# A transformer layer with routed attention and eight gated experts: the small LoRA product of the expert output moved behind the output matmuls

## The chip, the cores and the metric

The kernel runs on all 8 cores of one Trainium2 chip. Each core computes one of the eight sequences of the batch, 2048 tokens of width 1024, with the same program and no traffic between cores. The metric is the device time in microseconds of the slowest core.

## The reference

```python
x = x + attn(layernorm(x), ...)          # windowed light attention plus routed heavy attention
x = x + ffn(layernorm(x), Wg, W1, b1, A1, B1, W2, b2, A2, B2, W3, b3, A3, B3)

def ffn(x, ...):
    scores = softmax(xf @ Wg.T)
    expert_weights, expert_indices = top_k(scores, 2)   # normalised to sum 1
    gates = (one_hot(expert_indices, 8) * expert_weights[..., None]).sum(axis=1)
    h1 = lora_in(xf, W1, b1, A1, B1)     # xf @ W1^T + (xf @ A1^T) @ B1^T + b1, all 8 experts
    h3 = lora_in(xf, W3, b3, A3, B3)
    g = silu(h1) * h3
    y_e = lora_out(g, W2, b2, A2, B2)    # g @ W2^T + (g @ A2^T) @ B2^T + b2
    return einsum('te,ted->td', gates, y_e)
```

There are 8 experts with 2048 hidden units each, and every expert is computed for every token; the gates are zero for six of the eight. The rank of the LoRA parts is 16.

## The kernel before, in words

Everything is kept transposed, with features on the partitions and tokens along the free axis. Programs for the five engines are written out by hand: `P.do(engine, ...)` appends an instruction to that engine's queue, each engine runs its queue in order, and semaphores given as `waits` hold an instruction until another engine has counted up. With `drain=True` the next instruction of the same queue also waits for the end of this one. So the order in the text is the order on each engine.

The change lies in the last part, the expert stage (block "g"). Its outer loop `eq_i` runs over 32 quarters: 8 experts `e` with 4 quarters `q` of 512 hidden units each. The weights of a quarter (w1b, w3b, w2b, 1 MB each as bf16, and small LoRA pieces) are in two buffers that take turns; POOL's queue issues those of the next quarter when `mm4` says that the quarter that last used the buffer is done. In a quarter the loop `tc` runs over 4 chunks of 512 tokens. One pass of it is called a tile here; there are 128.

A tile does, in this order on TensorE:

- in quarter 0 only: the rank-16 products with A1 and A3 (`mku`, L1302) into rows 0 to 15 of the PSUM bank pMISC, which VectorE copies to u1sb and u3sb (L1315, L1320). The first of them waits for `vec3` among others.
- the gate matmul (L1324) into chunk 3 of pSIM. It waits for `oe`, that is for all sums into x1 so far. VectorE copies the result to gateb (L1330).
- four times (`hc`): a w1 group of eight matmuls and one for the LoRA part (`h13`, L1341 and L1346), and a w3 group of the same kind. ScalarE applies Silu to the one (L1356) and the bias to the other (L1365); VectorE multiplies them (L1370) and multiplies by gateb into gTq (L1376).
- the u2 product (`u2mm`, L1383): four matmuls of gTq with a2tqb, 16 wide, into rows 32 to 47 of pMISC. VectorE adds that to u2sb (L1391), which runs over the four quarters of an expert; in quarter 3 it is also copied to bf16 as u2bf (L1398).
- eight y groups (`ymm`, L1409): `dc` runs over the output features, 4 matmuls of w2b with gTq each, into chunks 0 and 1 of pSIM in turn. In quarter 3 each group has one more matmul that uses u2bf (L1415). After each group VectorE adds the chunk into x1 (L1432, "the sum into x1"); a y group waits until all but the last of these sums are done, by `oe`.

The first y group of every tile waits for `vec3`, so for the u2sb sum of its own tile. u2bf is read in quarter 3 alone.

Of the kernel before, what the change touches and what calls it, by code (L numbers as in the profile page):

```python
# [10 lines left out]
ALU = mybir.AluOpType  # L11
# [154 lines left out]
def build(debug_taps=()):  # L166
# [156 lines left out]
    u2sb = rowt("u2sb", 32, 0, 16, 2048, F32, ROWS)  # L323
    u2bf = rowt("u2bf", 0, 4096, 16, 2048, BF16, ROWS)
# [19 lines left out]
    pMISC = nc.alloc_psum_tensor("pMISC", [128, 512], F32)  # L344
# [8 lines left out]
    S = {k: Sem(nc, k) for k in names}  # L353
    nc.const_aps.register(F32, 1e-5, fconst[0:1, 0:1])
    P = Prog(nc, S)
# [27 lines left out]
    for _e in ("tensor", "vector", "scalar", "gpsimd"):  # L383
        P.do(_e, lambda E: E.nop(),
             waits=[(S["sdc"], SD_CONST), (S["sgc"], S["sgc"].n)])
# [41 lines left out]
    for dc in range(8):  # L427
# [3 lines left out]
             waits=ld + [(S["mm"], S["mm"].n)], inc=S["scl"], drain=True)  # L431
        def mk(d=dc):
            def f(E):
# [12 lines left out]
             inc=S["mm"])  # L446
# [5 lines left out]
    for dc in range(8):  # L452
# [3 lines left out]
             waits=ld + [(S["scl"], S["scl"].n),  # L456
                         (S["mm"], max(0, S["mm"].n - 1))],
             inc=S["vec"], drain=True)
        P.do("vector", (lambda d=dc: lambda E:
                        E.tensor_mul(xlch(d)[:, :], xlch(d)[:, :], rB[:, :]))(),  # L460
             inc=S["vec"], drain=True)
        P.do("scalar", (lambda d=dc: lambda E:
                        E.activation(xsq[:, :], xlch(d)[:, :], AF.Square))(),
             waits=[(S["vec"], S["vec"].n), (S["mm"], S["mm"].n)],
             inc=S["scl"], drain=True)
        def mk(d=dc):
# [19 lines left out]
         waits=[(S["mm"], S["mm"].n)], inc=S["vec"], drain=True)  # L486
    P.do("vector", lambda E: E.tensor_scalar_mul(c0_row, pSIM[0:1, 0:2048], 1 / 1024.0),
         inc=S["vec"], drain=True)
    P.do("vector", lambda E: E.tensor_copy(sr_row, pSIM[32:33, 0:2048]),
         inc=S["vec"], drain=True)  # L490
    P.do("vector", lambda E: E.tensor_mul(c1_row, c0_row, c0_row),
         inc=S["vec"], drain=True)
# [4 lines left out]
         waits=[(S["vec"], S["vec"].n)], inc=S["scl"], drain=True)  # L497
    P.do("scalar", lambda E: E.activation(sr_row, sr_row, AF.Sqrt),
         inc=S["scl"], drain=True)
    P.do("vector", lambda E: E.reciprocal(c1_row, t_row),  # L500
         waits=[(S["scl"], S["scl"].n)], inc=S["vec"], drain=True)
    P.do("vector", lambda E: E.tensor_scalar_max(sr_row, sr_row, 1e-12),
         inc=S["vec"], drain=True)
    P.do("vector", lambda E: E.reciprocal(sr_row, sr_row), inc=S["vec"], drain=True)
    P.do("vector", lambda E: E.tensor_scalar_mul(sr_row, sr_row, 32.0),
         inc=S["vec"], drain=True)
    P.do("vector", lambda E: E.tensor_mul(c0_row, c0_row, c1_row),
         inc=S["vec"], drain=True)
    P.do("vector", lambda E: E.tensor_scalar_mul(c0_row, c0_row, -1.0),
         inc=S["vec"], drain=True)  # L510
# [6 lines left out]
    for dc in range(8):  # L517
# [3 lines left out]
             waits=ld + [(S["scl"], S["scl"].n)], inc=S["vec"], drain=True)  # L521
        P.do("vector", lambda E: E.tensor_mul(xlt[:, :], xlt[:, :], rB[:, :]),
             inc=S["vec"], drain=True)
        P.do("vector", lambda E: E.tensor_mul(xlt[:, :], xlt[:, :], c1B[:, :]),
             inc=S["vec"], drain=True)
        P.do("vector", lambda E: E.tensor_add(xlt[:, :], xlt[:, :], c0B[:, :]),
             inc=S["vec"], drain=True)
# [4 lines left out]
             inc=S["vec"], drain=True)  # L532
    P.flush("p2b")
    if "ln2T" in debug_taps:
# [4 lines left out]
          inc=S["sgw"])  # L539
# [4 lines left out]
    for tt in range(16):  # L544
        def mk(tt=tt):
            def f(E):
# [10 lines left out]
             inc=S["mm"])  # L557
# [3 lines left out]
             waits=[(S["mm"], S["mm"].n)], inc=S["vec3"], drain=True)  # L561
# [3 lines left out]
             inc=S["vec2"], drain=True)  # L565
    for fc in range(8):
# [4 lines left out]
              waits=[(S["mm2"], max(0, S["mm2"].n - 4)), (S["mm"], S["mm"].n)],  # L571
              inc=wsem)
        sgn = wsem.n
        for tc in range(4):
            k = 4 * fc + tc
            def mk(fc=fc, tc=tc, k=k):
                def f(E):
# [12 lines left out]
                 inc=S["mm2"])  # L590
# [8 lines left out]
    if "lqkv" in debug_taps:  # L599
# [3 lines left out]
         waits=[(S["vec"], S["vec"].n)], inc=S["pool"], drain=True)  # L603
# [684 lines left out]
    for eq_i in range(32):  # L1288
# [7 lines left out]
        for tc in range(4):  # L1296
# [37 lines left out]
            for hc in range(4):  # L1334
# [3 lines left out]
                def h13(wb, btq, usb, bank, tc=tc, hc=hc):  # L1338
                    def f(E):
# [36 lines left out]
                                E.tensor_mul(gTq[:, 512 * hc:512 * hc + 512],  # L1376
                                             gtmp1[:, :], gateb[:, :]))(),
                     inc=S["vec"], drain=True)
            def u2mm(par=par):
                def f(E):  # L1380
                    ins = None
                    for hc in range(4):
                        ins = E.matmul(pMISC[32:48, 0:512],  # L1383
                                       a2tqb[par][:, 16 * hc:16 * hc + 16],
                                       gTq[:, 512 * hc:512 * hc + 512],
                                       start=(hc == 0), stop=(hc == 3))
                    return ins
                return f
            P.do("tensor", u2mm(), waits=[(S["vec"], S["vec"].n)], inc=S["mm2"])
            P.do("vector", (lambda tc=tc: lambda E:  # L1390
                            E.scalar_tensor_tensor(u2sb[:, 512 * tc:512 * tc + 512],  # L1391
                                                   pMISC[32:48, 0:512], 1.0,
                                                   u2sb[:, 512 * tc:512 * tc + 512],
                                                   ALU.mult, ALU.add))(),
                 waits=[(S["mm2"], S["mm2"].n)], inc=S["vec3"], drain=True)
            if q == 3:
                P.do("vector", (lambda tc=tc: lambda E:
                                E.tensor_copy(u2bf[:, 512 * tc:512 * tc + 512],  # L1398
                                              u2sb[:, 512 * tc:512 * tc + 512]))(),
                     inc=S["vec3"], drain=True)  # L1400
            GTC = S["vec"].n
            for dc in range(8):
                ybank = 0 if dc % 2 == 0 else 1
                def ymm(dc=dc, tc=tc, par=par, q=q, eq_i=eq_i, yb=ybank):
                    def f(E):
                        ins = None
                        for hc in range(4):
                            last = (hc == 3) and q != 3 and eq_i != 3
                            ins = E.matmul(pch(yb),  # L1409
                                           w2b[par][:, 1024 * hc + 128 * dc:  # L1410
                                                    1024 * hc + 128 * dc + 128],
                                           gTq[:, 512 * hc:512 * hc + 512],
                                           start=(hc == 0), stop=last)
                        if q == 3:
                            ins = E.matmul(pch(yb),  # L1415
                                           b2te[:, 128 * dc:128 * dc + 128],
                                           u2bf[:, 512 * tc:512 * tc + 512],
                                           start=False, stop=(eq_i != 3))
                        if eq_i == 3:
                            ins = E.matmul(pch(yb),  # L1420
                                           b2allb[:, 128 * dc:128 * dc + 128],
                                           gatesF[:, 512 * tc:512 * tc + 512],
                                           start=False, stop=True)
                        return ins
                    return f
                P.do("tensor", ymm(),
                     waits=[(S["vec"], GTC), (S["vec3"], S["vec3"].n),
                            (S["oe"], max(0, S["oe"].n - 1)),
                            (S["scl"], S["scl"].n), (S["scl2"], S["scl2"].n)],
                     inc=S["av"])  # L1430
                P.do("vector", (lambda dc=dc, tc=tc, yb=ybank: lambda E:
                                E.scalar_tensor_tensor(  # L1432
                                    x1[:, 2048 * dc + 512 * tc:
                                       2048 * dc + 512 * tc + 512],
                                    pch(yb), 1.0,
                                    x1[:, 2048 * dc + 512 * tc:
                                       2048 * dc + 512 * tc + 512],
                                    ALU.mult, ALU.add))(),
                     waits=[(S["av"], S["av"].n)], inc=S["oe"], drain=True)
        P.do("tensor", lambda E: E.nop(),  # L1440
             waits=[(S["scl"], S["scl"].n), (S["scl2"], S["scl2"].n),
                    (S["mm2"], S["mm2"].n), (S["av"], S["av"].n)],
# [36 lines left out]
```

How the kernel before makes its waits and increments, by code:

```python
                    def body(E):  # L145
                        seen = {}
                        prev_pend = [None]
                        for (waits, emit, inch, k, pend) in ops:
                            allw = list(waits)
                            if prev_pend[0] is not None:
                                allw.append(prev_pend[0])
                            for (s, n) in allw:
                                h = s.h
                                if seen.get(id(h), -1) < n:
                                    E.wait_ge(h, n)
                                    seen[id(h)] = n
                            ins = emit(E)
                            if inch is not None:
                                ins.then_inc(inch, k)
                            prev_pend[0] = (pend[0], pend[1]) if pend else None
```

## Time and profile before

| | us |
|---|---|
| median of 2 runs | 9090.02 (9080.91 to 9099.13) |
| the profiled execution | 8785.57 |
| its span, slowest core (core 2) | 8784.0 |
| its span, fastest core (core 7) | 8736.2 |
| expert stage in it (4142.5 to the end) | 4642 |

The profile is taken on the slowest core. Its page gives busy time by engine and by slices of the span; the trace behind it can be asked for waits (who stood idle, and whose end let it go on), for the instructions in order of time, and for the TensorE clock that was granted in a stretch (1.00 is 2.4 GHz, 0.50 is 1.2 GHz).

### The profile page before, as it was taken

The numbers are of one execution on the slowest core, as the hardware profiler recorded it, in microseconds if no ns is written. First come the engines' busy times: TensorE is split into PE (matmuls) and PEld (weight loads), VectorE is DVE, ScalarE is ACT, GpSimd is POOL, SyncE is SP. The second block draws the span as 40 slices with busy tenths as digits, with TensorE's granted clock in tenths as the row PEclk, the third lists the DMA queues.
The fourth block names the chain that finished last, engine by engine and source line by source line (L and its number), as shares of the span: only waits on it lengthen the run. The fifth ranks groups of instructions, "written<-read, shape, count | busy, mean of one in ns | idle before, by whom it ended". The sixth has DMA issues, their size and how long they took to land.

```text
span 8784.0 us, 70962 instructions; the slowest of 8 cores (8736.2 to 8784.0 us)
## 1 busy us (share of the span) xinstructions
PE 5469.5 (62%) x21893; PEld 2092.0 (24%) x22208; DVE 3297.3 (38%) x5936; ACT 1409.5 (16%) x1819; POOL 305.1 (3%) x335
## 2 busy tenths in 40 slices
PE   5221122245555555541888888888888888888887
PEld 1010000013333333210322322222223223232222
DVE  2732744474444444324322332323333323233322
ACT  1012000002222222111111111111111111111111
POOL 0022000000000000000000000000000000000000
PEclk8565555575555555675987989989999899899988
DMA  2100000010000000102011111121211021111110
GB/s 89 44 9 0 0 0 0 30 23 1 1 1 1 1 1 1 48 0 30 15 30 16 26 19 25 21 30 15 30 16 30 15 30 24 21 23 22 26 19 39
DMA packets 149539, 169.20 MB, mean 19 GB/s; under 512 B 55972, under 2 KB 125092, under 8 KB 142772
## 3 DMA queue, kind: packets, MB, share of 16 engines
q0 software_dynamic: 140512, 111.61, 8.7%
q1 hardware_dynamic: 8660, 53.04, 1.7%
q8 instruction: 189, 3.10, 0.1%
q14 instruction: 178, 1.46, 0.1%
HBM read 267.67 MB, written 8.39 MB: 31 GB/s over the span
## 4 chain that ended last, share of the span: by engine, by line
PE 43%; DVE 5%; issue 3%; ACT 1%; DMA 1%; DVEq 0%; POOL 0%; ACTq 0%; PEldq 0%; POOLq 0%
PE pSIM L1341 21%; PE pSIM L1409 12%; PE pSIM L1346 4%; DVE x L1432 2%; PE pMISC L1383 2%; PE pMISC L1302 2%; PE pSIM L1415 1%; ACT gtmp L1365 1%; DVE u2sb L1391 1%; DVE gtmp L1370 1%; DVE gTq L1376 1%; DMA b3ce<-b3c 1%; PE pSIM L1324 0%; DVEq L155 0%; DVE u1sb L1315 0%
## 5 line engine op out<-in xcount | busy, mean ns | idle before, releaser
L1409 PE MATMUL pSIM<-gTq,w2b 128*128 128x512 bf16 x4001 | 1236.0, 456 | 224.6 <-DVE u2sb L1391 125.6
L1432 DVE SCALAR_TENSOR_TENSOR x<-pSIM,x 128x512 f32<-128x512 f32 x1024 | 708.5, 692 | 837.3 <-PE pSIM L1409 491.3
L1341 PE MATMUL pSIM<-xl2T,w1b 128*128 128x512 bf16 x3989 | 977.3, 386 | 31.6 <-DVE u3sb L1320 23.2
L1341 PE MATMUL pSIM<-xl2T,w3b 128*128 128x512 bf16 x4005 | 971.5, 383 | 7.1 <-issue 3.5
L1370 DVE TENSOR_TENSOR gtmp<-gtmp,gtmp 128x512 bf16<-128x512 bf16 x512 | 217.8, 425 | 1893.7 <-ACT gtmp L1365 1893.7
L1356 ACT ACTIVATE gtmp<-pSIM,b1ce 128x512 bf16<-128x512 f32 x512 | 351.8, 687 | 3165.7 <-PE pSIM L1346 3147.3
L1409 PEld LDWEIGHTS pSIM<-gTq,w2b 128*128 128x128 bf16 x4096 | 396.7, 110 | 1019.6 <-issue 859.7
L969 PE MATMUL pT<-idbf,attnbf 128*128 128x128 bf16 x2048 | 259.0, 307 | 592.3 <-ACT attnbf L953 567.2
L1341 PEld LDWEIGHTS pSIM<-xl2T,w1b 128*128 128x128 bf16 x4096 | 362.7, 98 | 516.1 <-issue 172.6
L1341 PEld LDWEIGHTS pSIM<-xl2T,w3b 128*128 128x128 bf16 x4096 | 360.0, 98 | 485.3 <-issue 137.2
L1365 ACT ACTIVATE gtmp<-pSIM,b3ce 128x512 bf16<-128x512 f32 x512 | 352.0, 688 | 726.8 <-PE pSIM L1346 726.8
L940 DVE TENSOR_REDUCE smwk<-pSIM 128x1 f32<-128x512 f32 x512 | 354.2, 692 | 55.9 <-PE pSIM L924 2.3
L969 PEld LDWEIGHTS pT<-idbf,attnbf 128*128 128x128 bf16 x2048 | 198.4, 139 | 679.3 <-issue 679.3
L1383 PE MATMUL pMISC<-gTq,a2tqb 128*16 128x512 bf16 x512 | 170.7, 467 | 271.1 <-DVE gTq L1376 271.1
L953 ACT ACTIVATE attnbf<-pSIM,smwk 128x1024 bf16<-128x1024 f32 x128 | 142.6, 1114 | 1137.2 <-DVE smwk L949 1137.2
L757 PE MATMUL pT<-idbf,lattnT 128*128 128x128 bf16 x128 | 33.8, 264 | 426.9 <-DVE lattnT L752 426.9
L983 DVE COPY attnT<-pT 128x1024 bf16<-128x1024 bf16 x128 | 88.5, 692 | 497.1 <-PE pT L969 497.1
L995 PE MATMUL pOUT<-attnT,hv 128*65 128x128 bf16 x2048 | 245.0, 313 | 0.1
L1376 DVE TENSOR_TENSOR gTq<-gtmp,gateb 128x512 bf16<-128x512 bf16 x512 | 217.7, 425 | 53.3
L924 PE MATMUL pSIM<-hk,hq 64*128 64x512 bf16 x512 | 234.6, 609 | 4.7 <-DVE selqb L910 4.7
L995 PEld LDWEIGHTS pOUT<-attnT,hv 128*65 128x65 bf16 x2048 | 215.0, 174 | 19.0 <-issue 1.2
L413 PE MATMUL pSIM<-key_rt,ones_f 1*128 1x512 f32 x8 | 7.2, 1072 | 334.2 <-DVE zp_rt L646 334.2
(262 smaller groups left out, 4834.8 us busy)
## 6 DMA issues: line engine op xcount, KB each, us to landing
w1b<-w1q POOLq DMA_DIRECT2D x32, 1024.0 KB, 11.0
w3b<-w3q POOLq DMA_DIRECT2D x32, 1024.0 KB, 15.2
w2b<-w2q POOLq DMA_DIRECT2D x32, 1024.0 KB, 18.2
xs<-xT SPq DMA_DIRECT2D x24, 1024.0 KB, 4.9
xc<-xT SPq DMA_DIRECT2D x16, 1024.0 KB, 5.7
out<-x SPq DMA_DIRECT2D x8, 1024.0 KB, 10.4
wst<-wqkv POOLq DMA_DIRECT2D x8, 256.0 KB, 4.5
cos<-cos SPq DMA_DIRECT2D x1, 1024.0 KB
```

Source lines behind the costliest of these rows:

```text
L940: E.reduce_max(smwk[:, 2 + kc:3 + kc], pSIM[:, 512 * kc:512 * kc + 512], axis=AX.X))(),
L969: ins = E.transpose(pT[:, 1024 * half + 128 * (j - j0): 1024 * half + 128 * (j - j0) + 128], attnbf[:, 128 * j:128 * j + 128], idbf[:, :])
L995: ins = E.matmul(pOUT[0:65, 0:128], hv[:, 520 * j + 65 * h:520 * j + 65 * h + 65], attnT[:, 128 * j:128 * j + 128], start=(start and j == ...
L1341: E.matmul(pSIM[:, 512 * bank:512 * bank + 512], wb[:, 512 * dc + 128 * hc:512 * dc + 128 * hc + 128], xl2T[:, 2048 * dc + 512 * tc: 2048 ...
L1346: return E.matmul(pSIM[:, 512 * bank:512 * bank + 512], btq[:, 128 * hc:128 * hc + 128], usb[:, 512 * tc:512 * tc + 512], start=False, sto ...
L1356: E.activation(gtmp1[:, :], pSIM[:, 512 * b:512 * b + 512], AF.Silu, bias=b1ce[:, hcg:hcg + 1], scale=1.0))(),
L1365: E.activation(gtmp2[:, :], pSIM[:, 512 * b:512 * b + 512], AF.Identity, bias=b3ce[:, hcg:hcg + 1], scale=1.0))(),
L1370: P.do("vector", lambda E: E.tensor_mul(gtmp1[:, :], gtmp1[:, :], gtmp2[:, :]), waits=[(S["scl"], S["scl"].n), (S["scl2"], S["scl2"].n), ( ...
L1376: E.tensor_mul(gTq[:, 512 * hc:512 * hc + 512], gtmp1[:, :], gateb[:, :]))(),
L1383: ins = E.matmul(pMISC[32:48, 0:512], a2tqb[par][:, 16 * hc:16 * hc + 16], gTq[:, 512 * hc:512 * hc + 512], start=(hc == 0), stop=(hc == 3))
L1409: ins = E.matmul(pch(yb), w2b[par][:, 1024 * hc + 128 * dc: 1024 * hc + 128 * dc + 128], gTq[:, 512 * hc:512 * hc + 512], start=(hc == 0), ...
L1432: E.scalar_tensor_tensor(x1[:, 2048 * dc + 512 * tc: 2048 * dc + 512 * tc + 512], pch(yb), 1.0, x1[:, 2048 * dc + 512 * tc: 2048 * dc + 51 ...
```

## The change

In quarters 0, 1 and 2 the u2 product and the u2sb sum are issued behind the eight y groups and their sums into x1, and the y groups no longer wait for `vec3`. In quarter 3 they stay in front, with the wait. The u2 product keeps its count to wait for (`GTC`, the last gTq of its tile). The lines that follow move down: L1391 becomes L1394, L1409 becomes L1415, L1415 becomes L1421 and L1432 becomes L1438.

```diff
-            P.do("tensor", u2mm(), waits=[(S["vec"], S["vec"].n)], inc=S["mm2"])
-            P.do("vector", ... u2sb sum ...
-                 waits=[(S["mm2"], S["mm2"].n)], inc=S["vec3"], drain=True)
+            GTC = S["vec"].n
+
+            def emit_u2(tc=tc, par=par, q=q):
+                P.do("tensor", u2mm(par), waits=[(S["vec"], GTC)], inc=S["mm2"])
+                P.do("vector", ... u2sb sum ...
+                     waits=[(S["mm2"], S["mm2"].n)], inc=S["vec3"], drain=True)
+                if q == 3:
+                    P.do("vector", ... copy to u2bf ..., inc=S["vec3"], drain=True)
+
             if q == 3:
-                P.do("vector", ... copy to u2bf ..., inc=S["vec3"], drain=True)
-            GTC = S["vec"].n
+                emit_u2()
             for dc in range(8):
...
-                P.do("tensor", ymm(),
-                     waits=[(S["vec"], GTC), (S["vec3"], S["vec3"].n),
-                            (S["oe"], max(0, S["oe"].n - 1)),
-                            (S["scl"], S["scl"].n), (S["scl2"], S["scl2"].n)],
-                     inc=S["av"])
+                yw = [(S["vec"], GTC), (S["oe"], max(0, S["oe"].n - 1)),
+                      (S["scl"], S["scl"].n), (S["scl2"], S["scl2"].n)]
+                if q == 3:
+                    yw.append((S["vec3"], S["vec3"].n))
+                P.do("tensor", ymm(), waits=yw, inc=S["av"])
                 P.do("vector", ... sum into x1 ...)
+            if q != 3:
+                emit_u2()
```

On TensorE, between the first and the second tile of the first quarter 0 (the other quarters 0 are the same):

```order
 L1341 MATMUL pSIM<-xl2T,w3b_165 128x512 x8
 L1346 MATMUL pSIM<-u3sb,b3tqb_151 128x512
-L1383 MATMUL pMISC<-gTq,a2tqb_153 16x512 x4
-L1409 MATMUL pSIM<-gTq,w2b_167 128x512 x32
+L1415 MATMUL pSIM<-gTq,w2b_167 128x512 x32
+L1383 MATMUL pMISC<-gTq,a2tqb_153 16x512 x4
 L1302 MATMUL pMISC<-xl2T,a1te 16x512 x8
 L1302 MATMUL pMISC<-xl2T,a3te 16x512 x8
```

The u2 product stands behind the 32 matmuls of y, and directly in front of the a1 product of the next tile, which uses the same PSUM bank and waits for `vec3`.

On TensorE at the end of a tile of quarter 1, before:

```order
L1346 MATMUL pSIM<-u3sb,b3tqb_152 128x512
L1383 MATMUL pMISC<-gTq,a2tqb_154 16x512 x4
L1409 MATMUL pSIM<-gTq,w2b_168 128x512 x32
L1324 MATMUL pSIM<-gatesF,sel_55 128x512
L1341 MATMUL pSIM<-xl2T,w1b_164 128x512 x8
```

and after:

```order
L1346 MATMUL pSIM<-u3sb,b3tqb_152 128x512
L1415 MATMUL pSIM<-gTq,w2b_168 128x512 x32
L1383 MATMUL pMISC<-gTq,a2tqb_154 16x512 x4
L1324 MATMUL pSIM<-gatesF,sel_55 128x512
L1341 MATMUL pSIM<-xl2T,w1b_164 128x512 x8
```

Here the u2 product stands between the last y and the gate matmul.

On VectorE around the end of a tile of quarter 1, before:

```order
L1376 TENSOR_TENSOR gTq<-gtmp_121,gateb 128x512
L1391 SCALAR_TENSOR_TENSOR u2sb<-pMISC,u2sb 16x512
L1432 SCALAR_TENSOR_TENSOR x_111<-pSIM,x_111 128x512 x8
L1330 CAST gateb<-pSIM 128x512
L1370 TENSOR_TENSOR gtmp_121<-gtmp_121,gtmp_122 128x512
```

and after:

```order
L1376 TENSOR_TENSOR gTq<-gtmp_121,gateb 128x512
L1438 SCALAR_TENSOR_TENSOR x_111<-pSIM,x_111 128x512 x8
L1394 SCALAR_TENSOR_TENSOR u2sb<-pMISC,u2sb 16x512
L1330 CAST gateb<-pSIM 128x512
L1370 TENSOR_TENSOR gtmp_121<-gtmp_121,gtmp_122 128x512
```

The u2sb sum stands between the last sum into x1 and the gateb copy of the next tile. ScalarE's and POOL's instructions are in the same order in both kernels.

## Rows read from the trace of the kernel before

**Rows 1.** Page: busy tenths in 40 slices, and the last chain by line.
```profile
PE   5221122245555555541888888888888888888887
...
DVE  2732744474444444324322332323333323233322
...
PE pSIM L1341 21%; PE pSIM L1409 12%; PE pSIM L1346 4%; DVE x L1432 2%; PE pMISC L1383 2%; PE pMISC L1302 2%; PE pSIM L1415 1%; ACT gtmp L1365 1%; DVE u2sb L1391 1%; DVE gtmp L1370 1%; DVE gTq L1376 1%; DMA b3ce<-b3c 1%; PE pSIM L1324 0%; DVEq L155 0%; DVE u1sb L1315 0%
```

**Rows 2.** Spans and mean granted clock, slowest and fastest core.
```profile
core 2: 8784.0 us, clock 0.737
...
core 7: 8736.2 us, clock 0.740
```

**Rows 3.** TensorE's waits, 4142.5 to 8785: total us, times, longest us.
```profile
PE pMISC L1383 <- DVE gTq L1376: 271.1, 128, 2.5
PE pSIM L1409 <- DVE u2sb L1391: 125.6, 96, 2.0
PE pSIM L1324 <- DVE x L1432: 98.0, 96, 1.4
PE pSIM L1409 <- DVE u2bf L1398: 59.2, 32, 2.5
```

**Rows 4.** Timeline around one tile's end: start, us, instruction, [idle before <-releaser].
```profile
5727.72 1.02 PE L1383 MATMUL pMISC<-gTq,a2tqb 128*16 128x512 bf16 x4 [2.11 <-DVE gTq L1376]
5728.92 0.68 DVE L1391 SCALAR_TENSOR_TENSOR u2sb<-pMISC,u2sb 16x512 f32<-16x512 f32 x1 [1.35 <-PE pMISC L1383]
...
5729.97 2.72 PE L1409 MATMUL pSIM<-gTq,w2b 128*128 128x512 bf16 x6 [1.22 <-DVE u2sb L1391]
...
5739.66 0.69 DVE L1432 SCALAR_TENSOR_TENSOR x<-pSIM,x 128x512 f32<-128x512 f32 x1 [0.48 <-PE pSIM L1409]
...
5740.49 0.37 PE L1324 MATMUL pSIM<-gatesF,sel 8*128 8x512 bf16 x1 [1.01 <-DVE x L1432]
...
5740.80 1.90 PE L1341 MATMUL pSIM<-xl2T,w1b 128*128 128x512 bf16 x8
5741.04 0.69 DVE L1330 CAST gateb<-pSIM 128x512 bf16<-128x512 f32 x1 [0.69 <-PE pSIM L1324]
...
5742.95 0.39 PE L1341 MATMUL pSIM<-xl2T,w3b 128*128 128x512 bf16 x1
```

**Rows 5.** Stretches: us, busy of five engines (count), granted clock, DMA share, GB/s.
```profile
4142.50:8785.00 4642.50, 3901.03 (x14442) 1333.98 (x14735) 1387.61 (x2405) 705.07 (x1025) 153.90 (x215) 0.89 0.15 23
...
5475.60:5607.40 131.80, 111.87 (x428) 39.76 (x437) 41.25 (x72) 22.00 (x32) 4.34 (x7) 0.92 0.16 25
5607.40:5740.50 133.10, 113.00 (x428) 40.02 (x437) 41.23 (x72) 22.00 (x32) 4.37 (x7) 0.91 0.16 25
...
8464.30:8614.10 149.80, 131.06 (x428) 42.88 (x437) 41.25 (x72) 21.99 (x32) 4.05 (x6) 0.76 0.13 22
8464.30:8487.40 23.10, 20.90 (x72) 6.96 (x74) 4.09 (x9) 5.50 (x8) 4.05 (x6) 0.81 0.85 139
...
5730.00:5733.50 3.50, 3.28 (x9) 1.28 (x11) 0.69 (x1) 0.00 (x0) 0.00 (x0) 0.56 0.00 0
...
5738.00:5740.50 2.50, 1.34 (x7) 0.36 (x5) 1.69 (x3) 0.00 (x0) 0.29 (x1) 1.00 0.00 0
```

**Rows 6.** Timeline of TensorE in a tile that keeps its clock.
```profile
6034.07 1.02 PE L1383 MATMUL pMISC<-gTq,a2tqb 128*16 128x512 bf16 x4 [2.11 <-DVE gTq L1376]
6036.31 1.89 PE L1409 MATMUL pSIM<-gTq,w2b 128*128 128x512 bf16 x7 [1.22 <-DVE u2sb L1391]
...
6045.68 0.37 PE L1324 MATMUL pSIM<-gatesF,sel 8*128 8x512 bf16 x1 [1.01 <-DVE x L1432]
```

**Rows 7.** Timeline where a tile of quarter 0 follows another.
```profile
6007.97 1.02 PE L1409 MATMUL pSIM<-gTq,w2b 128*128 128x512 bf16 x4
...
6008.93 1.89 PE L1302 MATMUL pMISC<-xl2T,a1te 128*16 128x512 bf16 x8
6009.17 0.69 DVE L1432 SCALAR_TENSOR_TENSOR x<-pSIM,x 128x512 f32<-128x512 f32 x1 [0.48 <-PE pSIM L1409]
```

More of the change, by code:

```diff
@@ L1378, in build, with u2mm @@
                      inc=S["vec"], drain=True)
-            def u2mm(par=par):
+            def u2mm(par):
                 def f(E):
@@ L1388, in u2mm @@
                 return f
-            P.do("tensor", u2mm(), waits=[(S["vec"], S["vec"].n)], inc=S["mm2"])
[L1390 to L1394, printed above, removed]
-                 waits=[(S["mm2"], S["mm2"].n)], inc=S["vec3"], drain=True)
-            if q == 3:
[L1397 to L1400, printed above, removed]
-            GTC = S["vec"].n
+            GTC = S["vec"].n
+            def emit_u2(tc=tc, par=par, q=q):
+                P.do("tensor", u2mm(par), waits=[(S["vec"], GTC)], inc=S["mm2"])
+                P.do("vector", (lambda tc=tc: lambda E:
+                                E.scalar_tensor_tensor(
+                                    u2sb[:, 512 * tc:512 * tc + 512],
+                                    pMISC[32:48, 0:512], 1.0,
+                                    u2sb[:, 512 * tc:512 * tc + 512],
+                                    ALU.mult, ALU.add))(),
+                     waits=[(S["mm2"], S["mm2"].n)], inc=S["vec3"], drain=True)
+                if q == 3:
+                    P.do("vector", (lambda tc=tc: lambda E:
+                                    E.tensor_copy(u2bf[:, 512 * tc:512 * tc + 512],
+                                                  u2sb[:, 512 * tc:512 * tc + 512]))(),
+                         inc=S["vec3"], drain=True)
+            if q == 3:
+                emit_u2()
             for dc in range(8):
```

## The prediction

> **What bounds the kernel now.** I read the page first. From slice 20 of its 40 slices on TensorE is busy about eight tenths and VectorE two to four, and the chain that ended last runs mostly over TensorE, by the expert stage's lines L1341, L1409, L1346, L1383 and over the sum into x1, L1432 [rows 1]. The slowest core spans 8784.0 us and the cores agree within 0.6%, so one stands for all [rows 2]. Then TensorE's list of waits over the expert stage, 4142.5 to 8785: its two largest are both around the small u2 product. It waits for the last gTq in front of L1383, 271.1 us in 128 times, and for the u2sb sum in front of L1409, 125.6 us in 96 times [rows 3]. The 96 are the tiles of quarters 0 to 2 (8 experts x 3 quarters x 4 token chunks), which are the tiles that the change touches. Third is the wait of the next tile's gate matmul for the last sum into x1, 98.0 us, 96 times.
>
> The timeline of one tile (gate matmul at 5708.0) shows the order: last w3 group until 5725.6 (u2 starts at 5727.72 after 2.11 idle), idle 2.11 while ScalarE and VectorE finish gTq, u2 product at 5727.72, idle 1.22 for the u2sb sum, first y at 5729.97, eight y groups, last sum into x1 at 5739.66, next gate at 5740.49 [rows 4]. Last I read the granted clock by stretches. It is 1.00 (2.4 GHz) up to the u2 product (its four matmuls take 1.02 us in this tile and in that of [rows 6]), falls to 1.2 GHz behind it (the mean of 5730 to 5733.5 is 0.56, and L1409 needs 2.72 us for six matmuls there), and is 1.00 again at the tile's end [rows 4, 5]. In another tile it didn't fall: first y 6036.31, next gate 6045.68 [rows 6]. So the gap around u2 costs twice: its own length, and a y stage at the lower clock behind it.
>
> **The change, part by part.** In quarters 0 to 2 the four u2 matmuls and the u2sb sum move behind the eight y groups, and y no longer waits for the sum. In quarter 3 all stays.
>
> *In front of y, 96 tiles.* The first y now starts where L1383 did: 5729.97 - 5727.72 = 2.25 us earlier [rows 4], and 6036.31 - 6034.07 = 2.24 in the other tile [rows 6]. The wait for gTq in front of it stays (2.11 us), since y reads gTq too; it is what is late next. 96 x 2.25 = 216 us.
>
> *Behind y, 72 tiles that are followed by a gate matmul.* The four u2 matmuls take about 4 x 0.22 = 0.9 us at 2.4 GHz. They start when the last y ends, and TensorE already stands idle 1.01 us there until the last sum into x1 is done, as the gate matmul waits for it in both kernels [rows 4, 6]. That idle time hides them, with about 0.1 us to spare; without the cover they would cost 0.9. The u2sb sum (0.68 us) is then queued on VectorE between the last sum into x1, done at 5740.35, and the gateb copy: it would run to about 5741.13 and the copy (0.69) to about 5741.9, where it ended at 5741.73. The first that needs gateb is the w3 group, behind a w1 group, at 5742.95, and so isn't held [rows 4]. Cost 0. From both sides: nothing, or 0.3 us x 72 = 22 us if u2 ends late.
>
> *Behind y, 24 tiles of quarter 0 that are followed by the a1 product of the next chunk.* Before, a1 follows the last y without a gap: L1409 at 6007.97 for 1.02, L1302 at 6008.93 [rows 7]. Now it waits for the u2sb sum, because both use pMISC. The last sum into x1 ends at 6009.86, the u2sb sum after it takes 0.68 and some 0.1 to start, and a matmul starts 0.37 after such a sum (5729.60 to 5729.97, [rows 4]): a1 at about 6011.0, 2.1 us later than before. 24 x 2.1 = 50 us are given back. Queued behind the waiting a1 is all of TensorE's work; VectorE waits for a1.
>
> *The clock.* Mean length of a tile of quarters 1 and 2 of one expert: (131.8 + 133.1) / 8 = 33.1 us [rows 5]; 21.95 us from the gate to the first y (5708.0 to 5729.97), so y to the next gate takes 11.15. It takes 9.37 where the clock stays at 2.4 GHz [rows 6], 10.52 where it falls briefly (5729.97 to 5740.49) [rows 4], and the mean says that longer falls are common. The lower clock thus costs some 1.8 us a tile. No row shows the new gap. The nearest on one side is the old gap, 2.11 idle, 1.0 of work, 1.22 idle: the clock falls after it. On the other side is the idle 1.01 in front of the gate matmul, after which it stays (1.00 in 5738 to 5740.5) [rows 5]. The new one, 2.11 idle and then full work, lies between. I take half of the tiles without a fall and half with the short one: 9.37 + 0.5 x 1.15 = 9.95, a gain of 1.2 x 96 = 115 us. Ends: nothing (every tile falls as now) and 1.8 x 96 = 173 us (none falls).
>
> Sum: 216 - 50 + 115 = 281 us, ends 216 - 50 - 22 = 144 and 216 - 50 + 173 = 339.
>
> *Which time it is taken from.* The profiled execution took 8785.57 us, so the sum gives 8505 for such a run. The two runs shown are 9081 to 9099, median 9090.02: 304 us or 3.5% more. One state in the trace could make this: from 8464.3 on the slowest core was granted 0.81, and the four tiles to 8614.1 took 149.8 us (mean 0.76, with the falls in them), 37.45 each, 4.3 more than 33.1 [rows 5]; 304 / 4.3 = 71 tiles in it would do. That is an estimate; the trace can't tell. The gap in front of u2 is set by ScalarE and VectorE and not by that clock, so I take the same 281 us off: 9090 - 281 = 8809.
>
> The Trainium skill ("TensorE: Matmul & The Clock Gate", section "Seeing it yourself") says that a current limit takes a die to 13/16 of the clock once three of its cores run dense matmuls, and holds it while the load lasts. This case's trace agrees on the level, 0.81, but shows it for a short stretch only, with the mean of the expert stage at 0.89, falls to 1.2 GHz included. By the rule all 128 tiles would be in it before and after, and the gain would be about the same; but a kernel with fewer gaps is denser, which is the third rival.
>
> **Rivals.**
>
> *1. The clock still falls in every tile as now.* For: even two idle pieces of 2.1 and 1.2 with work between them bring it down nearly always, and the larger piece stays. Against: between the pieces only 1.0 us of work stood, now full work follows at once. Gain 216 - 50 = 166 us: 8924.
>
> *2. It falls in none.* For: tiles exist that didn't fall with the whole gap [rows 6]. Against: those are few, by the mean of 11.15 against 9.37. Gain 339 us: 8751.
>
> *3. The denser kernel sits longer at the 0.81 clock (the slower side).* Place: the w1 and w3 groups, whose pitch goes from 0.22 to 0.26 us. Price 4.3 us a tile [rows 5]. It eats the 281 us from 66 more tiles on. If 71 tiles are in it already, the other 57 cost 245 us: 9054, within 2%. If the 304 us come from something else and 124 tiles are new in it, 533 us: 9342. For: TensorE's share of work in a tile rises by some 12%. Against: quarters with TensorE busy 85% of the time (111.87 of 131.8 us) show a mean of 0.92, which leaves no room for it [rows 5], and the cores differ little [rows 2].
>
> That the change doesn't do what it says is no rival: the order of TensorE's instructions shows u2 behind y, and the wait of y for the u2sb sum is gone.
>
> **How the numbers follow.** Forecast 0.66, rival 1 0.14, rival 2 0.12, rival 3 0.08, half of it slower. A measurement of this kernel tells about 2% (182 us) from no change. Faster by over 2%: forecast, rival 2, and a little of rival 1 where some tiles keep the clock, 0.66 + 0.12 + 0.02 = 0.80. Slower by over 2%: half of rival 3, 0.04. Within 2%: 0.16. The range reaches from 8700 (339 us, and another 0.3 us x 96 for y stages a little shorter than 9.37, 368 us in all, rounded down) to 8950 (the low end of the sum, 144 us, gives 8946).
>
> **What would show it.** Right: TensorE's wait for u2sb in front of y is gone in 96 tiles and only the one for u2bf (32 times, 59.2 us [rows 3]) stays; the wait for gTq, about 200 us, stands in front of y instead of in front of u2; a new wait for u2sb stands in front of L1302, at most 2.1 us in each of 24 times; the mean clock of the expert stage is over 0.89 and its length about 4643 - 281 = 4362 us; tiles of quarters 1 and 2 take 29.0 to 30.5 us. Wrong: a mean clock that stays at 0.89 or below (rival 1), a gate matmul that starts later than 1.0 us after the last y, or much more time at 0.81 (rival 3).

## The result, and the profile after

| | before | changed |
|---|---|---|
| median of all runs, us | 8914.52 (10 runs, 8779.12 to 9099.13) | 8582.01 (11 runs, 8549.66 to 8839.43) |
| profiled execution, span of the slowest core, us | 8784.0 | 8560.0 |
| expert stage in it, us | 4642 | 4421 |

The ratio is 0.9735, 95% interval 0.9692 to 0.9778: 2.65% faster. In the profiled executions it is 224 us, 221 of them in the expert stage. The forecast said faster by 281 us and a time of 8809 in a range of 8700 to 8950. The direction came out and the mechanism in kind; the gain was 0.8 of the forecast, and the time is below the range. In some executions of either kernel the cores of one die, or of both, are granted a lower clock (in the changed kernel's run of 8839 us 0.711 against 0.747 on the other die), and the ratios here are of the executions without that, so they differ from the ratio of the medians in the table. The two runs of before that were at hand for the prediction, 9081 and 9099, are the longest of its ten; the shortest four are 8779 to 8794.

TensorE's waits in the expert stage of the changed kernel (total us, times, longest us), beside [rows 3]:

```profile
PE pSIM L1415 <- DVE gTq L1376: 224.7, 96, 2.7
PE pMISC L1383 <- DVE gTq L1376: 67.9, 32, 2.5
PE pSIM L1415 <- DVE u2bf L1402: 49.5, 32, 1.9
...
PE pMISC L1302 <- DVE u2sb L1394: 26.7, 24, 1.1
PE pSIM L1324 <- DVE x L1438: 25.5, 27, 1.0
```

The 96 waits of y for the u2sb sum are gone and only the 32 for u2bf are left. The wait for gTq stands in front of y in 96 tiles, at 224.7 / 96 = 2.34 us each, where in front of u2 it was 271.1 / 128 = 2.12. The wait for u2bf in quarter 3, which should have stayed as it was, fell from 59.2 to 49.5 us; the experiment on the waits of y says why. The new wait in front of a1 (L1302) is there, 24 times, 1.1 us each. And the gate matmul's wait for the last sum into x1 shrank from 98.0 us in 96 times to 25.5 in 27: that is the idle time in which u2 now hides.

TensorE's timeline of the changed kernel at the end of a tile of quarter 2, and where a tile of quarter 0 follows another (beside [rows 4, 7]):

```profile
5557.66 1.02 PE L1415 MATMUL pSIM<-gTq,w2b 128*128 128x512 bf16 x4
5558.61 1.03 PE L1383 MATMUL pMISC<-gTq,a2tqb 128*16 128x512 bf16 x4
5559.70 0.37 PE L1324 MATMUL pSIM<-gatesF,sel 8*128 8x512 bf16 x1
5560.00 1.90 PE L1341 MATMUL pSIM<-xl2T,w1b 128*128 128x512 bf16 x8
...
5871.17 1.89 PE L1415 MATMUL pSIM<-gTq,w2b 128*128 128x512 bf16 x8 [2.33 <-DVE gTq L1376]
...
5879.10 1.03 PE L1383 MATMUL pMISC<-gTq,a2tqb 128*16 128x512 bf16 x4
5881.24 1.89 PE L1302 MATMUL pMISC<-xl2T,a1te 128*16 128x512 bf16 x8 [1.11 <-DVE u2sb L1394]
```

In front of the gate matmul nothing is idle any more. In quarter 0 a1 starts 5881.24 - 5879.10 = 2.14 us behind the start of u2, and before it started there itself: the 2.1 us that the prediction gives back.

The stretches of the changed kernel: the expert stage, then quarters 1 and 2 of the third expert (us, busy of five engines, granted clock, DMA share, GB/s), beside [rows 5]:

```profile
4138.70:8560.00 4421.30, 3859.36 (x14737) 1320.20 (x14736) 1387.64 (x2406) 705.06 (x1025) 153.89 (x215) 0.91 0.15 24
5409.00:5529.40 120.40, 109.36 (x437) 38.98 (x437) 41.29 (x73) 22.00 (x32) 4.33 (x6) 0.96 0.17 27
5529.40:5652.10 122.70, 110.88 (x436) 39.03 (x437) 41.19 (x73) 22.00 (x32) 4.34 (x6) 0.94 0.17 27
```

The two quarters take (120.4 + 122.7) / 8 = 30.4 us a tile; they took 33.1, and the sum of the prediction makes 33.1 - 2.25 - 1.2 = 29.65 of them. The granted clock rose from 0.92 and 0.91 to 0.96 and 0.94, not to 1.00. So the clock still falls in these tiles, for a shorter time. That is the open point with which the experiments began.

### The profile page after: what moved, and what is told of

The parts are those of the page before. It is cut to its first block, busy times and chain, and to the rows that moved or that the text cites. A ratio compares the mean times of both kernels' runs of the same rounds, so it can differ in the third digit from the quotient of the medians.

```text
span 8560.0 us, 71205 instructions; the slowest of 8 cores (8515.9 to 8560.0 us)
## 1 busy us (share of the span) xinstructions
PE 5425.2 (63%) x22208; PEld 2076.7 (24%) x22208; DVE 3296.0 (39%) x5936; ACT 1409.5 (16%) x1819; POOL 305.1 (4%) x335
## 4 chain that ended last, share of the span: by engine, by line
PE 43%; DVE 4%; issue 2%; ACT 1%; DMA 1%; POOL 0%; DVEq 0%; ACTq 0%; PEldq 0%; POOLq 0%
PE pSIM L1341 22%; PE pSIM L1415 12%; PE pSIM L1346 4%; PE pMISC L1302 2%; PE pMISC L1383 2%; DVE x L1438 2%; PE pSIM L1421 1%; ACT gtmp L1365 1%; DVE gtmp L1370 1%; DVE gTq L1376 1%; DMA b3ce<-b3c 1%; DVE u2sb L1394 0%; PE pSIM L1324 0%; DVE u3sb L1320 0%; DVE u1sb L1315 0%
## 5 line engine op out<-in xcount | busy, mean ns | idle before, releaser
L1415 PE MATMUL pSIM<-gTq,w2b 128*128 128x512 bf16 x4096 | 1196.8, 440 | 305.5 <-DVE gTq L1376 224.7
L1341 PE MATMUL pSIM<-xl2T,w1b 128*128 128x512 bf16 x4096 | 999.9, 388 | 21.0 <-DVE u3sb L1320 21.0
L1438 DVE SCALAR_TENSOR_TENSOR x<-pSIM,x 128x512 f32<-128x512 f32 x1024 | 708.0, 691 | 767.3 <-PE pSIM L1415 450.8
L1341 PE MATMUL pSIM<-xl2T,w3b 128*128 128x512 bf16 x4096 | 980.0, 382 | 0.0
L1415 PEld LDWEIGHTS pSIM<-gTq,w2b 128*128 128x128 bf16 x4096 | 385.1, 107 | 1039.7 <-issue 852.5
L1341 PEld LDWEIGHTS pSIM<-xl2T,w1b 128*128 128x128 bf16 x4096 | 364.1, 99 | 520.0 <-issue 179.5
L1341 PEld LDWEIGHTS pSIM<-xl2T,w3b 128*128 128x128 bf16 x4096 | 359.7, 98 | 485.8 <-issue 136.4
L1346 PE MATMUL pSIM<-u1sb,b1tqb 16*128 16x512 bf16 x512 | 200.0, 391 | 0.0
```

The source lines that it names most:

```text
L1341: E.matmul(pSIM[:, 512 * bank:512 * bank + 512], wb[:, 512 * dc + 128 * hc:512 * dc + 128 * hc + 128], xl2T[:, 2048 * dc + 512 * tc: 2048 ...
L1346: return E.matmul(pSIM[:, 512 * bank:512 * bank + 512], btq[:, 128 * hc:128 * hc + 128], usb[:, 512 * tc:512 * tc + 512], start=False, sto ...
L1415: ins = E.matmul(pch(yb), w2b[par][:, 1024 * hc + 128 * dc: 1024 * hc + 128 * dc + 128], gTq[:, 512 * hc:512 * hc + 512], start=(hc == 0), ...
L1438: E.scalar_tensor_tensor(x1[:, 2048 * dc + 512 * tc: 2048 * dc + 512 * tc + 512], pch(yb), 1.0, x1[:, 2048 * dc + 512 * tc: 2048 * dc + 51 ...
```

## The experiments

All ratios are to the kernel before on the same chip. "Unused matmuls" are extra ones whose result nobody reads; apart from them the experiments compute the same as the kernel. Each kernel has one traced execution, of all eight cores. Where the ratios can't tell two kernels apart, the lengths of the tiles in these traces are compared: from a tile's gate matmul to that of the next tile, as the median of the eight cores.

### Only the wait goes, u2 stays in front: e1_wait_only and e9_wait_only_again

```diff
 # kernel before
-                P.do("tensor", ymm(), waits=[(S["vec"], GTC), (S["vec3"], S["vec3"].n), ...
+                yw = [(S["vec"], GTC), (S["oe"], max(0, S["oe"].n - 1)), ...
+                if q == 3:
+                    yw.append((S["vec3"], S["vec3"].n))
+                P.do("tensor", ymm(), waits=yw, inc=S["av"])
```

> The u2 product stays in front of y; only the wait of y for the u2sb sum is taken away in quarters 0 to 2. Theory (the gain of the change is idle time in front of y, plus a clock that falls for a shorter time because that idle time is shorter): 96 x 1.22 us = 117 us of wait go, nothing is given back in quarter 0, and the clock part is like that of the change, some 70 us: 187 us in all, ratio 0.979 to before. Rival (the clock part needs the u2 product itself out of the way): 117 us alone, ratio 0.987, with the mean granted clock as before.

Its four runs gave no ratio: median 8636.75 (8535.54 to 8691.67), the profiled one 8535.5. So it ran again, with the changed kernel beside it.

> The wait-only kernel (u2 stays in front of y, y doesn't wait for the u2sb sum in quarters 0 to 2), which had one undisturbed run, 8535.5. Theory (the move gives y 1.1 us in 96 tiles but lets the clock fall more often and gives back 2.1 us in 24 tiles): as fast as the changed kernel or up to 0.4% faster, ratio 0.970 to 0.974. Rival (that run was a stray, and the u2 product in front of y costs its 1 us x 72 after all): 0.980 or more.

> The changed kernel itself once more, as the comparison for the wait-only kernel on the same chip: ratio 0.9735 within 0.4%.

The wait-only kernel: 0.9735 (0.9635 to 0.9834), lowest run 8529.7. The changed kernel: 0.9721 (0.9609 to 0.9833), lowest run 8552.6. The ratios can't tell them apart, and both are as expected of the second batch; the first expectation, 0.979, was too little. So moving the u2 product bought nothing over taking the wait away. Where its 1 us in front of y went is seen in the first wait-only run (u2, y, next gate; then quarters 1 and 2 of the third expert):

```profile
5557.39 1.02 PE L1383 MATMUL pMISC<-gTq,a2tqb 128*16 128x512 bf16 x4 [2.11 <-DVE gTq L1376]
5558.35 1.90 PE L1409 MATMUL pSIM<-gTq,w2b 128*128 128x512 bf16 x8
...
5567.55 0.37 PE L1324 MATMUL pSIM<-gatesF,sel 8*128 8x512 bf16 x1 [1.01 <-DVE x L1432]
```

```profile
5414.20:5537.70 123.50, 109.17 (x436) 38.29 (x437) 41.24 (x72) 22.05 (x32) 4.33 (x7) 0.96 0.18 27
5537.70:5659.90 122.20, 107.89 (x436) 37.92 (x437) 41.25 (x72) 22.05 (x32) 4.32 (x7) 0.97 0.18 27
```

y starts 0.96 us behind u2 instead of 2.25, without any idle time between. These quarters take (123.5 + 122.2) / 8 = 30.7 us a tile, against 30.4 with the move, at a slightly higher clock (0.96 and 0.97 against 0.96 and 0.94). The 0.3 us x 72 = 22 us that the move gains there are less than the 24 x 2.1 = 50 us that it gives back in quarter 0. The traces say the same over all 96 tiles of quarters 0 to 2: 3044 us for the wait-only kernel, 3073 for the changed one. They also say why the move gains 0.3 us there and not the 1 us that u2 takes: with u2 in front of y the clock falls less often. In 41 to 50 of the 96 y stages, by core, it doesn't fall at all, in the changed kernel in 14 to 20.

### The idle time filled: e3_after_fill, e4_before_fill and e6_fill4

```diff
+            def fill(par=par):
+                def f(E):
+                    ins = None
+                    for i in range(8):
+                        ins = E.matmul(pMISC[64:128, 0:512], w1b[par][:, 64 * i:64 * i + 64],
+                                       xl2T[:, 512 * i:512 * i + 512], start=True, stop=True)
+                    return ins
+                return f
+            if q != 3:
+                P.do("tensor", fill())
```

This stands behind the last w3 group of a tile. In the kernel before it is in front of u2, and four more are behind u2; with 4 in place of 8 it is the last of the three.

> The changed kernel with eight more matmuls (512 columns, result unused) in the remaining idle time in front of y in quarters 0 to 2. They need 1.7 of its 2.1 us. Theory (the idle time is what makes the clock fall behind it): the clock stays at 2.4 GHz in these 96 tiles, y to next shrinks from 10.5 to about 9.2 us, 96 x 1.1 = 105 us less than the changed kernel: ratio about 0.962. Rival (the fall has another cause, or the extra work costs clock elsewhere): 0.9735 or more, with falls in three tiles of four as before.

> The kernel before with eight unused matmuls in front of the u2 product and four behind it, in quarters 0 to 2. All waits stay. Theory (the idle pieces around u2 make the clock fall, which costs 1.8 us a tile): 96 x 1.8 = 173 us less than before, ratio 0.980. Rival (the fall has another cause): no change, ratio 1.00.

> The changed kernel with four unused matmuls (0.9 us) in front of y in quarters 0 to 2 in place of eight, so that about 1.4 us stay idle. Theory (how far the clock falls depends on how much of the stretch is idle, and the idle 1.0 us in front of the gate matmul never makes it fall): no fall or few, ratio 0.958 to 0.962. Rival (any idle time above 1 us in front of y brings it down): falls in most tiles, ratio 0.970 or more.

Measured: 0.9577 (0.9514 to 0.9640) for the changed kernel with eight, 0.9621 (0.9568 to 0.9673) with four, 0.9737 (0.9673 to 0.9800) for the kernel before with eight and four. The first and the third gained more than expected. All three held the clock: in 90 to 96 of the 96 y stages, by core, it doesn't fall. Quarters 1 and 2 of the third expert in the three profiles, one fence each in that order (changed with eight, changed with four, before with eight and four):

```profile
5377.70:5493.80 116.10, 110.96 (x458) 40.55 (x469) 41.26 (x73) 21.99 (x32) 4.33 (x6) 1.00 0.20 28
5493.80:5610.70 116.90, 110.94 (x460) 40.63 (x469) 41.26 (x73) 21.99 (x32) 4.33 (x6) 1.00 0.20 28
```

```profile
5375.70:5491.80 116.10, 108.25 (x453) 38.80 (x453) 41.26 (x73) 22.02 (x32) 4.33 (x6) 1.00 0.18 28
5491.80:5608.60 116.80, 108.27 (x453) 38.88 (x453) 41.27 (x73) 22.01 (x32) 4.34 (x6) 1.00 0.18 28
```

```profile
5408.70:5532.40 123.70, 114.99 (x475) 41.98 (x485) 41.26 (x72) 21.98 (x32) 4.26 (x7) 1.00 0.16 26
5532.40:5656.80 124.40, 114.77 (x475) 42.01 (x484) 41.26 (x72) 21.98 (x32) 4.31 (x7) 1.00 0.16 26
```

The column to read is the granted clock, 1.00 in all six. More work on TensorE made the kernel faster, with every wait left in place in the third: so the falls come from the idle time around u2 and not from load. With these rows the tile's gain can be split, in us for the eight tiles of the two quarters: before 264.9, before with the clock held 248.1, changed 243.1, changed with the clock held 233.0. The lower clock costs (264.9 - 248.1) / 8 = 2.1 us a tile before and (243.1 - 233.0) / 8 = 1.3 after; with the clock held the edit is worth (248.1 - 233.0) / 8 = 1.9. The gain of 2.7 us is 1.9 of wait and 0.8 of clock. All 64 tiles of quarters 1 and 2 give nearly the same: 33.17, 31.00, 30.38 and 29.06 us a tile, so 2.2 of clock before, 1.3 after, 1.9 of wait. The unused matmuls aren't quite neutral: the y stages in which the clock doesn't fall by itself take 9.3 us on the mean and with them 9.1 to 9.2, so each price of the clock may be 0.1 to 0.2 too high. Four unused matmuls do what eight do (2957 and 2958 us for the 96 tiles), so idle time of some 2.34 - 0.9 = 1.4 us in front of y doesn't bring the clock down in these tiles, and 2.34 does in four of five.

### The wait of a1: e2_a1_free and b1_fill_a1

```diff
+            VEC3A = S["vec3"].n            # behind the memset of u2sb, ahead of the loop over tc
...
-                            (S["vec3"], S["vec3"].n), (S["vec"], S["vec"].n),
+                            (S["vec3"], VEC3A), (S["vec"], S["vec"].n),
```

The first is the changed kernel with this alone, the second has the eight unused matmuls as well.

> The changed kernel, but the a1 product of token chunks 1 to 3 of quarter 0 doesn't wait for the u2sb sum. Theory (24 tiles give back 2.1 us because a1 waits for that sum): a1 starts right behind the u2 product, 0.9 us instead of 2.1 behind the last y, 24 x 1.2 = 30 us less than the changed kernel, ratio about 0.970 to before. Rival (something else holds TensorE there, so the wait only changes its name): the same as the changed kernel, 0.9735.

> The changed kernel with both: eight unused matmuls in front of y in quarters 0 to 2, and an a1 product that doesn't wait for the u2sb sum. Theory (the clock part and the give-back in quarter 0 are independent): the 24 x 2.1 = 50 us of a1's wait come off the 8436 us of the kernel with the unused matmuls alone: about 8386, ratio 0.952. Rival (they share a cause, the idle time behind y): less than 20 us off, ratio 0.956 or more.

Measured: 0.9648 (0.9599 to 0.9696), where the changed kernel has 0.9735, and with the unused matmuls 0.9537 (0.9506 to 0.9568), where they alone have 0.9577. In the profiled executions the first is 8560.0 - 8495.5 = 64.5 us shorter and not 30. Its 24 tiles of quarter 0 take 34.51 us each, 2.1 less than the changed kernel's 36.59, which is 50 of these us; the other tiles hardly differ. The lowest run of the second, on another chip, is 8381.0, 55.5 below 8436.5, near the 50 expected. The wait is real and its cost doesn't depend on the clock, but more than the 1.2 us expected of the first has gone. TensorE's timeline shows what (a2tqb is u2, a1te is a1):

```profile
5854.72 1.89 PE L1416 MATMUL pSIM<-gTq,w2b 128*128 128x512 bf16 x8
5856.53 0.38 PE L1384 MATMUL pMISC<-gTq,a2tqb 128*16 128x512 bf16 x1
5856.55 0.38 PE L1303 MATMUL pMISC<-xl2T,a1te 128*16 128x512 bf16 x1
5856.75 0.38 PE L1384 MATMUL pMISC<-gTq,a2tqb 128*16 128x512 bf16 x1
5856.77 0.38 PE L1303 MATMUL pMISC<-xl2T,a1te 128*16 128x512 bf16 x1
5856.97 0.38 PE L1384 MATMUL pMISC<-gTq,a2tqb 128*16 128x512 bf16 x1
5856.98 0.38 PE L1303 MATMUL pMISC<-xl2T,a1te 128*16 128x512 bf16 x1
```

The two 16-wide products run side by side: each pair starts 0.01 to 0.02 us apart, and a pair takes 0.22 us, as long as one. All four u2 matmuls stand ahead of a1 in TensorE's queue, and yet a1's first starts before u2's second; so where no wait stands between, the order in the text isn't quite the order on the engine, which the description of the kernel before takes it to be. So a1 starts where u2 does, 2.1 us earlier than with the wait, and u2 costs no time of its own there: 24 x 2.1 = 50 us.

### Where the move alone stands when the clock is held: e5_wait_fill

The wait-only kernel with the eight unused matmuls in front of u2.

> The u2 product stays in front of y, y doesn't wait for the u2sb sum, and eight unused matmuls stand in front of u2 (quarters 0 to 2). With the clock held in both, this against the changed kernel with unused matmuls (8436) prices the move of u2 alone. Theory: y starts 1.1 us later in 96 tiles, of which the idle time in front of the next gate matmul had hidden nothing, and the 2.1 us of a1's wait in 24 tiles are not given back: 0.6 us x 72 = 43 us more, 1.4 us x 24 = 33 us less, ratio within 0.3% of 0.958. Rival (the move is what the gain consists of): 70 us or more slower than it, ratio 0.966.

Its six runs (8469.6 to 8958.3, median 8688.0) gave no ratio, and the profiled one, 8469.6, is 33 us above the 8436.5 of the changed kernel with the same filling, between the two expectations (10 and 70). The traces decide it, as the clock is held in both. A tile of quarters 1 and 2 takes 29.71 us against 29.06 with the move, 0.65 more; one of the 24 of quarter 0 takes 34.17 against 35.64, 1.5 less. Over the 96 tiles that is 2967 against 2958 us: 9 us for the move, as the theory had it (10). On the slowest core of this execution the clock was 0.81 in 4 of the 64 y stages of quarters 1 and 2, which is part of the 33 us.

### The waits of y: e7_one_wait

```diff
 # changed kernel
-                yw = [(S["vec"], GTC), (S["oe"], max(0, S["oe"].n - 1)),
-                      (S["scl"], S["scl"].n), (S["scl2"], S["scl2"].n)]
+                yw = [(S["vec"], GTC), (S["oe"], max(0, S["oe"].n - 1))]
```

> The changed kernel, but y doesn't wait for ScalarE's two semaphores, which the gTq count implies. In the changed kernel the first y starts 0.23 us later behind gTq than the u2 product did (idle 2.34 against 2.11 us). Theory (each semaphore that TensorE's queue has to look at takes time, and the u2 product had one where y has three): the idle time in front of y is 2.11 to 2.2 us, 96 x 0.15 to 0.23 = 14 to 22 us less than the changed kernel. Rival (the wide weight load or the first y itself makes the difference): 2.34 as before.

Its waits in the expert stage:

```profile
PE pSIM L1415 <- DVE gTq L1376: 203.0, 96, 2.5
```

203.0 / 96 = 2.11 us, where it was 2.34. The two semaphores had been counted up before, and still the wait in front of y was 0.23 us longer for them, 22 us over 96 tiles. The lower of its two runs is 8545.7, 4 us below the lowest of the changed kernel, and there is no ratio; but the tiles are shorter, 3049 us for the 96 against 3073, of which 22 are the wait. So the effect is shown in the trace, and its rival (the weight load or y itself) falls.

It is the place in the list that costs, not the number. In this kernel every semaphore of `waits` becomes a wait instruction of its own in front of the matmul, in the order of the list; one whose count was already waited for is left out. In quarters 0 to 2 ScalarE's two stand behind the one that comes last, gTq's. In quarter 3 the edit happened to change the order: before, `vec3` stood ahead of ScalarE's two, and now it is appended behind them. The copy to u2bf and the first y of a tile of quarter 3, before and in the changed kernel, one fence each:

```profile
5798.31 0.41 DVE L1398 CAST u2bf<-u2sb 16x512 bf16<-16x512 f32 x1
5799.09 1.87 PE L1409 MATMUL pSIM<-gTq,w2b 128*128 128x512 bf16 x4 [1.74 <-DVE u2bf L1398]
```

```profile
5712.17 0.41 DVE L1402 CAST u2bf<-u2sb 16x512 bf16<-16x512 f32 x1
5712.73 1.86 PE L1415 MATMUL pSIM<-gTq,w2b 128*128 128x512 bf16 x4 [1.52 <-DVE u2bf L1402]
```

y starts 0.37 us behind the end of the copy before and 0.15 now, with the same semaphores in the list. To name the semaphore that comes last at the end of the list would thus do what e7_one_wait does; that wasn't run.

### The fastest: b2_fill_q3 and b3_fill_q3_one_wait

```diff
 # b1_fill_a1, in quarter 3 too: fill() ahead of u2, and
+                if q == 3 and dc == 0:
+                    P.do("tensor", ymm(tail=False), waits=yw[:-1])
+                    P.do("tensor", ymm(dc=1, yb=1, tail=False), waits=[(S["oe"], S["oe"].n)])
+                if q == 3 and dc < 2:
+                    P.do("tensor", ymm(base=False), waits=yw[-1:], inc=S["av"])
+                else:
+                    P.do("tensor", ymm(), waits=yw, inc=S["av"])
```

`base` is the four matmuls of w2b, `tail` the narrow ones that follow (u2bf, and in expert 0 b2allb).

> As the last one, and in quarter 3 too: the unused matmuls in front of u2, and the first two y groups issue their four matmuls of w2b behind u2 at once and only their u2bf matmul waits for the u2bf copy. Theory: in 28 tiles the wait of 1.5 us goes and a fall of the clock that costs some 2.5 us, 112 us; in the 4 tiles of expert 0, where the whole y stage runs at 1.2 GHz (23.3 us), another 4 x 10 us: in all some 150 us, ratio 0.935. Rival (in quarter 3 the clock stays down for another reason, such as the narrow 16-row matmuls in each y group): only the waits go, 32 x 1.5 = 48 us, ratio 0.947.

> The fastest so far (unused matmuls in all quarters, a1 free, first two y groups of quarter 3 split), with y waiting for the gTq count alone as in the last one. Theory: 128 x 0.15 us = 20 us less than its 8228, ratio 0.933 to 0.934. Rival: 0.936 as before.

Measured: 0.9358 (0.9328 to 0.9388), lowest run 8228.1, and 0.9335 (0.9255 to 0.9415), lowest 8220.7. The first is as expected; the second isn't told from the first, so its 20 us aren't shown. Against the kernel without the edit in quarter 3 the lowest runs give 8381.0 - 8228.1 = 153 us; 150 were expected. Quarter 3 of expert 0 before and in this kernel, one fence each:

```profile
4551.80:4756.80 205.00, 176.47 (x506) 47.73 (x516) 45.35 (x78) 22.00 (x32) 11.76 (x17) 0.68 0.17 23
```

```profile
4498.30:4647.80 149.50, 134.38 (x548) 45.58 (x548) 45.71 (x79) 21.99 (x32) 12.10 (x17) 0.98 0.22 29
```

Its four tiles took 205.0 us at a mean clock of 0.68 and take 149.5 at 0.98, with more matmuls in them. The rival (narrow matmuls keep the clock down there) falls. Within this edit the share of the split and that of the filling weren't tried apart.

### The tiles of the kernels side by side

Median of the eight cores of the traced execution, us. The third column has the tiles of quarter 0 that another of quarter 0 follows; "no fall" counts the y stages of the 96 (first y to next gate matmul) with a mean granted clock over 0.99, lowest and highest core; the few that the filled kernels lack were for the most part at 0.81.

| kernel | tile, quarters 1 and 2 | tile, quarter 0 | the 96 tiles | no fall |
|---|---|---|---|---|
| before | 33.17 | 37.52 | 3293 | 3 to 7 |
| changed | 30.38 | 36.59 | 3073 | 14 to 20 |
| wait only (e1) | 30.67 | 34.77 | 3044 | 41 to 50 |
| changed, one wait (e7) | 30.06 | 36.45 | 3049 | 21 to 29 |
| changed, a1 free (e2) | 30.37 | 34.51 | 3018 | 18 to 23 |
| before, filled (e4) | 31.00 | 35.53 | 3092 | 91 to 96 |
| wait only, filled (e5) | 29.71 | 34.17 | 2967 | 92 to 96 |
| changed, filled (e3) | 29.06 | 35.64 | 2958 | 96 |
| changed, filled with four (e6) | 29.06 | 35.63 | 2957 | 90 to 96 |

## Why the prediction was right or wrong

**Which time it is taken from: the step that put the time outside the range.** The prediction saw that the profiled execution (8785.57) was 304 us shorter than the two timed runs and took its sum off the timed ones, 9090. They turned out to be the longest of ten, and the shortest four lie at 8779 to 8794, with the profiled one. From that one the sum gives 8505, 0.7% below the 8561 of the changed kernel's profiled execution, and the same ends (144 and 339) give 8447 to 8642, which holds the 8582. Its likely cause for the 304 us, a lower clock in the two runs, can't be shown for them: no clock of theirs is on record. The unfounded part was that the changed kernel's runs would be compared with times like these two: two runs and a profile that disagree by more than the expected gain left both bases open.

**The clock, 1.2 x 96 = 115 us: the step of the sum that failed.** It said that half of the tiles would keep the clock, that a fall costs 1.15 us, and that the lower clock costs 1.8 in all. The clock is kept in 14 to 20 of the 96 y stages, not in 48. A tile of quarters 1 and 2 lost 2.2 us to it before and loses 1.3 now, so 0.9 came back and not 1.2. Over the 96 tiles, by the kernels with the clock held, that is 3293 - 3092 = 201 us before and 3073 - 2958 = 115 after: 86 us. The value was put midway between two bounds, the old gap that makes the clock fall and an idle 1.0 us that doesn't; the new gap of 2.34 us is in fact on the side of the old one in most tiles. The row for the second bound (5738 to 5740.5) ends where the gate matmul starts; that the clock stays behind it too is in [rows 4], where eight matmuls of L1341 take 1.90 us. Nothing in the trace of before could place the new gap closer, which was a reason to give the case between forecast and rival 1 more weight.

**In front of y, 96 x 2.25 = 216 us: right in kind, a little too much.** The wait for the u2sb sum went in all 96 tiles. But behind the wait for gTq stand two more in front of y that u2 didn't have, and it takes 2.34 us where u2's took 2.11: 2.02 a tile, 194 us. The priced value with the clock held, 1.9, agrees.

**Behind y, 72 tiles, nothing: right.** u2 stands in the former idle time in front of the gate matmul (5558.61, gate at 5559.70), and the gate's wait fell from 98.0 to 25.5 us.

**Behind y, 24 tiles, 2.1 us each given back: right**, 2.14 in the timeline. With the clock held these tiles take 35.64 us against 35.53 before, so what y gained in front is given back behind. It was seen only as the price of the wait; that u2 and a1 could have run side by side, so that nothing need be given back, wasn't seen.

**Quarter 3, where "all stays": not quite.** Moving `vec3` to the end of the list starts y 0.22 us earlier in 32 tiles, 7 of the 9.7 us by which the wait for u2bf fell.

Summed again with the clock held: 3092 - 2958 = 134 us of waits, where the sum had 216 - 50 = 166 and the traces of the waits 194 - 50 = 144, and 86 of clock, where it had 115: 220 us in the 96 tiles of the median core. On the slowest cores, which the pages show, the stage became 221 us shorter, 209 in the 96 tiles and 12 in quarter 3. The two quarters of one expert alone would give 194 - 50 + 0.8 x 96 = 221 us; that this meets the stage to the microsecond is luck.

Of the signs named ahead, the waits, the new wait of a1 (1.1 us, 24 times) and a mean clock over 0.89 (0.91) came out; the stage, 4421 us, is 59 longer than the 4362 named, and the slowest core's tiles of quarters 1 and 2, 30.7 us, are just above the 29.0 to 30.5.

**Rival 1** (the clock falls as now, 166 us) is nearer than was thought: 224 us is about halfway between it and the forecast. **Rival 2** (no falls) is refuted. **Rival 3** (the denser kernel sits longer at 0.81) is refuted: the mean clock of the eight cores rose (core 2 from 0.737 to 0.748), and kernels that are denser still kept 1.00.

## What to carry to other kernels

A TensorE that stands idle for two microseconds in every tile can lose more in the clock behind the idle time: here 2.34 us idle cost another 1.3 on average. So read the granted clock by stretches behind each wait, and price it by filling the gap with unused matmuls, which is a few lines and a fix at once. Before an instruction is moved off the critical path, try taking away only the wait that it caused: here this gave the whole gain, and the move's own share was given back where the next user of its PSUM bank waited for it. In a list of waits put the semaphore that comes last at the end. And when a profiled execution and the timed runs differ by more than the expected gain, the range has to hold both.

## What the runs showed of the hardware

- Four unused matmuls (0.9 us) in an idle time of 2.34 us hold the clock at 2.4 GHz in nearly every tile (90 to 96 of the 96 y stages, by core); without them it falls in 76 to 82, and the mean of two quarters is 0.94 to 0.96. Eight matmuls in front of u2 and four behind it hold it in the kernel before too, where it falls in 89 to 93.
- The wait-only kernel holds its clock better than the changed one (no fall in 41 to 50 of the 96 y stages against 14 to 20). Its idle time is 2.11 us in front of u2 against 2.34 in front of y, but that is a small part of it: in e7_one_wait y has the 2.11 too, and the count is 21 to 29. What else makes the difference stays open.
- Two wait instructions on semaphores that are already counted up cost TensorE 0.22 us when they stand behind the wait that ends last (0.37 us from the end of u2bf to y in the kernel before, and 2.34 against 2.11 us idle in e7_one_wait), and nothing when they stand ahead of it (0.15 us in quarter 3 of the changed kernel).
- Two 16-wide products into rows 0 to 15 and 32 to 47 of one PSUM bank run at the same time in e2_a1_free, 0.22 us a pair. The Trainium skill ("TensorE: Matmul & The Clock Gate", section "Part 3: Packing small matmuls — row/col tiling") says that matmuls at different tile positions of the array overlap; this trace agrees, with starts 0.01 to 0.02 us apart, and it happened without being asked for, as soon as no wait stood between them.
